# Second attention layer of a graph network: scores turned first, border rows stored by SyncE, queries spread as two float32r parts

## The reference, cut to what matters

```python
xn = _layernorm(x, ln1_g, ln1_b)
q = (xn @ Wq + bq).reshape(n, H, DH)
k = (xn @ Wk + bk).reshape(n, H, DH)
v = (xn @ Wv + bv).reshape(n, H, DH)
ep = ef @ We + be
scores = jnp.einsum('ehd,ehd->eh', q[dst], k[src] + ep[:, None, :]) * scale
scores = scores * ew[:, None]
m = jax.ops.segment_max(scores, dst, num_segments=n)
ex = jnp.exp(scores - m[dst])
s = jax.ops.segment_sum(ex, dst, num_segments=n)
attn = ex / s[dst]
out = jax.ops.segment_sum(attn[:, :, None] * v[src], dst, num_segments=n)
```

## Time and profile before

| what | value |
|---|---|
| time, median of 3 (lowest, highest) | 7788.41 us (7787.7, 7788.8) |
| profiled execution, span from first to last instruction | 7783.9 us |
| busy in the span: PE, DVE, ACT, POOL | 73%, 61%, 47%, 67% |
| granted TensorE clock, mean of the span | 0.852 |

### The profile page before, as it was taken

The page is one execution under the profiler, slowest core; times in us unless marked ns, Lnnn a source line. Parts: engine busy times, 40 slices in busy tenths (PEclk is TensorE's granted clock), DMA queues, the critical chain, the costliest instruction groups (busy, mean ns, idle before and its releaser), DMA issues. The chain is left out here.

```text
span 7783.9 us, 119247 instructions
## 1 busy us (share of the span) xinstructions
PE 5677.2 (73%) x30906; PEld 4272.7 (55%) x30906; DVE 4785.2 (61%) x14720; ACT 3689.1 (47%) x11072; POOL 5222.5 (67%) x5181
## 2 busy tenths in 40 slices
PE   6777765555568989968999999798555555667764
PEld 5666665555545666645666666565433434545543
DVE  8666666666657888867889898411222223555555
ACT  1333332222257777745777787342000002777774
POOL 4777777777777777734777777211777773777773
PEclk9777787777789999988999999898777777888787
DMA  4333241111156665546666666322444443444444
GB/s 148 79 76 81 77 107 36 37 36 33 36 125 154 159 159 154 156 114 167 190 187 188 186 190 177 111 66 78 109 109 108 109 108 72 110 110 110 109 109 89
DMA packets 1041439, 886.68 MB, mean 114 GB/s; under 512 B 748889, under 2 KB 857457, under 8 KB 1040663
## 3 DMA queue, kind: packets, MB, share of 16 engines
q0 software_dynamic: 259600, 658.46, 30.8%
q1 hardware_dynamic: 725907, 162.47, 10.7%
q10 hardware_dynamic: 55284, 58.13, 2.2%
HBM read 737.69 MB, written 140.99 MB: 113 GB/s over the span
## 5 line engine op out<-in xcount | busy, mean ns | idle before, releaser
L1282 POOL DMA_INDIRECT edges_kv<-kv,edges_rec x1712 | 1882.4, 1100 | 639.2 <-issue 525.9
L1428 PE MATMUL banks<-edges_kv,edges_hot 128*128 128x288 f32 (+2 forms) x5136 | 1484.8, 438 | 322.7 <-DVE edges_kv L1752 234.1
L1428 PEld LDWEIGHTS banks<-edges_kv,edges_hot 128*128 128x128 f32 x5136 | 1030.9, 209 | 605.8 <-issue 336.2
L1943 POOL DMA_INDIRECT edges_rows<-rel,edges_rec x856 | 809.5, 946 | 382.2 <-issue 255.6
L572 POOL DMA_INDIRECT by_src_records<-sort_by_src_rec,sort_by_src_pos_i x808 | 795.5, 985 | 325.6 <-issue 226.5
L1282 POOL DMA_INDIRECT edges_kv<-feat,edges_rec x856 | 828.9, 968 | 268.5 <-issue 245.2
L1959 PE MATMUL banks<-edges_rows,edges_hot 128*128 128x256 f32 x1712 | 625.0, 529 | 467.7 <-DMA edges_rows<-rel,edges_rec 431.3
L572 POOL DMA_INDIRECT by_dst_records<-sort_by_dst_rec,sort_by_dst_pos_i x808 | 787.6, 975 | 246.4 <-issue 243.6
L659 DVE SCALAR_TENSOR_TENSOR sort_junk<-banks,sort_hot_lo 128x128 bf16<-128x128 f32 x1616 | 437.9, 287 | 654.5 <-PE banks L721 638.6
L1959 PEld LDWEIGHTS banks<-edges_rows,edges_hot 128*128 128x128 f32 x1712 | 429.6, 263 | 663.5 <-DMA edges_rows<-rel,edges_rec 269.3
L1582 ACT ACTIVATE edges_off<-columns,edges_column 128x128 bf16<-128x128 f32 x2568 | 785.6, 393 | 0.0
(11 more groups left out here) (433 smaller groups left out, 11669.2 us busy)
## 6 DMA issues: line engine op xcount, KB each, us to landing
edges_kv<-kv,edges_rec POOLq DMA_INDIRECT x1712
sort_feat<-in_edge_attr_dram SPq DMA_DIRECT2D x100, 256.0 KB, 4.0
rel<-tables_stage SPq DMA_DIRECT2D x100, 252.0 KB
by_dst_records<-by_dst_blank ACTq DMA_DIRECT2D x21, 800.0 KB
edges_rec<-by_dst_records SPq DMA_DIRECT2D x26, 640.0 KB, 7.0
by_src_records<-by_src_blank ACTq DMA_DIRECT2D x1, 13696.0 KB, 52.6
edges_rows<-rel,edges_rec POOLq DMA_INDIRECT x856, 2.7
edges_kv<-feat,edges_rec POOLq DMA_INDIRECT x856
```

Of the source, the lines that this page charges most:

```text
L1282: pool.indirect_dma_start(kv[:, r, c, 0:koff + DIM], None, tab, bass.IndirectOffsetOnAxis(ap=reci[:, b, c, idx:idx + 1], axis=0)).then_inc ...
L1428: last = pe.matmul(ps[:, 6 + m % 2, 0:OW], hot[:, b % 2, c, :], kv[:, b % BUFS, c, koff:koff + OW], start=(c % 2 == 0), stop=(kind != 1 an ...
L1943: pool.indirect_dma_start(rows[:, r, c, :], None, tab, bass.IndirectOffsetOnAxis(ap=reci[:, b, c, idx:idx + 1], axis=0)).then_inc(gathered ...
```

## The change

Three things change in the second layer, and some tiles share memory to make place for them.

1. TensorE's `body` turns the scores of the step before first, then does `with_past` of pair 3 (of three steps before; it was the last thing of the body of the step ahead), and then `expand` of pair 2.
2. Border rows are stored in every step by SyncE (`store_ends`), `STORE_LAG` = 9 steps behind the step for which it loads; `HELD` is 2 for this layer. ScalarE waits, ahead of a step's first pair, for the store of two steps earlier.
3. Queries come in two parts: `q_high`, with the low 12 bits of each word cleared, and the rest in `x`. `hot_t` is float32r, and `expand` makes two float32r products per tile, one with each part, into the same PSUM columns. `join_and_project` makes the parts, two VectorE instructions more per block.

Beside that, records are loaded with 37 words in place of 40, five small tiles of the layer lie in `by_src.cont_all`, tiles of the joining part lie in `h` and `hn`, and `acc1` lies in the memory of `acc0`.

```diff
+F32R = mybir.dt.float32r
+HIGH_BITS = -(1 << 12)
...
-    RW = O.width - word0
+    RW = (O.words["weight"] + 1 if kind == 1 else O.width) - word0
...
-    HOT = F32 if kind < 3 else BF16
+    HOT = (F32, F32R, None, BF16)[kind]
...
-    HELD = 4
+    HELD = 2 if kind == 1 else 4
+    STORE_LAG = 9
...
+                ends_rows = C.ends[0:T, 0:OW].rearrange("(i q) w -> q i w", q=2)
+
+                def store_ends(j, b):
+
+                    sp.wait_ge(sums_copied, at(j, b)(PAIRS, PAIRS))
+                    sp.dma_start(ends_rows[:, bass.ds(at(j, b)(PAIRS, 0), PAIRS), :],
+                                 pair_sums[BN:P, b % HELD]).then_inc(ends_kept[b % HELD], 16)
 
                 def body(j, b):
+                    load(j, b)
+                    stored = before(j, b, STORE_LAG)
+                    if kind == 1 and stored:
+                        store_ends(*stored)
+
+                def load(j, b):
...
-                        rows = q[:, bass.ds(blocks[m], 1), :].rearrange("p o w -> p (o w)")
+                        rows = [part[:].bitcast(F32R)[:, bass.ds(blocks[m], 1), :].rearrange("p o w -> p (o w)") for part in q]
...
                         for c in range(2):
-                            last = pe.matmul(out[:, c, :], hot_t[:, b % 2, 2 * m + c, :], rows, start=True, stop=True,
-                                             skip_group_check=True)
+                            for part in range(2):
+                                last = pe.matmul(out[:, c, :], hot_t[:, b % 2, 2 * m + c, :], rows[part], start=(part == 0), stop=(part == 1),
+                                                 skip_group_check=True)
...
+                    gone = lagging(j, b, 3)
+                    if older:
+                        turn_scores(*older)
+                    if gone:
+                        with_past(*gone, 3)
                     if inside:
                         expand(j, b, (2,))
-                    if older:
-                        turn_scores(*older)
...
-                    if oldest and kind == 1:
-                        with_past(*oldest, 3)
...
-                    if 0 in pairs and b % HELD == 0:
+                    if kind == 1 and 0 in pairs and not first_steps(j, b, HELD):
+                        act.wait_ge(ends_kept[b % HELD], (j * (UNROLL // HELD) + b // HELD) * 16)
+                    if kind != 1 and 0 in pairs and b % HELD == 0:
                         act.wait_ge(ends_out, j * (UNROLL // HELD * 16) + b // HELD * 16)
...
-                    if PAIRS - 1 in pairs and (b % HELD == HELD - 1 or b == size(j) - 1):
+                    if kind != 1 and PAIRS - 1 in pairs and (b % HELD == HELD - 1 or b == size(j) - 1):
...
                     dve.tensor_tensor(x[:, b, :], ps[:, Q_BANK[b % 2], 0:DIM], bias[:, KV:KV + DIM], ALU.add).then_inc(q_kept, 1)
+                    dve.wait_ge(q_kept, b + 1)
+                    dve.tensor_scalar(q_high[:, b, :].bitcast(I32), x[:, b, :].bitcast(I32), HIGH_BITS, None, ALU.bitwise_and).then_inc(q_cut, 1)
+                    dve.wait_ge(q_cut, 2 * b + 1)
+                    dve.tensor_tensor(x[:, b, :], x[:, b, :], q_high[:, b, :], ALU.subtract).then_inc(q_cut, 1)
```

More of the change, by code:

```diff
@@ L1100, in blocks_of, with edge_layer @@
     return [((word >> (5 * m)) & 31).with_bounds(min_val=0, max_val=NB - 1) for m in range(PAIRS)]
-def edge_layer(nc, C, L, label, tab, q, acc, w_attr=None, beside=None):
+def edge_layer(nc, C, L, label, tab, q, acc, w_attr=None, beside=None, spare=None):
     kind, H, O, koff = L.kind, L.heads, L.order, L.koff
@@ L1188, in edge_layer @@
         pen = ph.sbuf("pen", [HG, 3, P + 1])
[L1189 to L1193, removed]
+        names = ("run_max", "seg_max", "last_max", "below", "expo")
+        run_max, seg_max, last_max, below, expo = (spare[0:HG, P * i:P * i + P] if spare else ph.sbuf(name, [HG, P])
+                                                   for i, name in enumerate(names))
         score = ph.sbuf("score", [P, G, H])
@@ L1236, in edge_layer @@
         ends_out = ph.sem("ends_out")
+        ends_kept = [ph.sem(f"ends_kept{i}") for i in range(HELD)] if kind == 1 else None
         added = ph.sem("added")
@@ L1256, in body @@
                     sp.dma_start(rec[:, b:b + some].rearrange("p s c w -> p (s c) w"),
-                                 records[:, bass.ds(j * (UNROLL * G) + b * G, some * G), word0:O.width]).then_inc(rec_in[b // LOAD], 16)
+                                 records[:, bass.ds(j * (UNROLL * G) + b * G, some * G), word0:word0 + RW]).then_inc(rec_in[b // LOAD], 16)
                     if beside and (j, b) == (1, 0):
@@ L1268, in _ @@
                 steps(sp, body)
+                if kind == 1:
+                    for n in range(STEPS - STORE_LAG, STEPS):
+                        store_ends(n // UNROLL, n % UNROLL)
+                    for i in range(HELD):
+                        sp.wait_ge(ends_kept[i], 16 * len(range(i, STEPS, HELD)))
                 if beside:
@@ L2062, in split_tiles, with split_views @@
         self.node_row = sbuf("node_row", [P, TB * P])
+    def split_views(self, L, first, second, sbuf):
+        H, n = L.heads, TB * P
+        self.cont_pen, self.max_row = first[0:H, 0:n + 1], first[0:H, n + 1:2 * n + 1]
+        self.run_max, self.node_row = second[0:H, 0:n], second[:, n:2 * n]
+        self.factor = sbuf("factor", [P, TB, H])
+        self.below = sbuf("below", [P, TB, H])
 FAR_BANKS = (3, 6, 7)
@@ L3278, in build @@
         far0, far1, far3 = (far for _, far in C.far_tables)
-        H0 = 16
-        kv0 = table("kv0", NR, P + DIM)
-        L = Layer(0, H0, by_src, P, P)
-        with nc.sbuf_tensor("acc0", [P, NB, L.out_width], F32) as acc:
+        H0, H1 = 16, 8
+        kv0, kv1 = table("kv0", NR, P + DIM), table("kv1", NR, 2 * DIM)
+        x_kept, h_kept = (nc.dram_tensor(name, (P, NB, DIM), F32, kind="Internal").ap() for name in ("x1_kept", "h1_kept"))
+        L0, L1 = Layer(0, H0, by_src, P, P), Layer(1, H1, by_dst, DIM, DIM)
@@ L3285, in build @@
+        with nc.sbuf_tensor("acc0", [P, NB, L0.out_width], F32) as acc0:
+            acc1 = acc0[:].rearrange("p b w -> p (b w)")[:, 0:NB * L1.out_width].rearrange("p (b w) -> p b w", b=NB)
             with nc.sbuf_tensor("q0", [P, NB, P], F32) as q, nc.sbuf_tensor("w_attr", [P, 2, 2 * P], F32) as w_attr:
[L3286 removed]
+                sort_all(nc, C, A, x, by_src, by_dst, table("edge_projected", E, 32), kv0, q, acc0, w_attr,
@@ L3296, in build @@
-        L = Layer(1, H1, by_dst, DIM, DIM)
-        with nc.sbuf_tensor("acc1", [P, NB, L.out_width], F32) as acc:
-            edge_layer(nc, C, L, "edges1", kv1, x, acc)
+                edge_layer(nc, C, L0, "edges0", kv0, q, acc0, w_attr, by_dst)
+            with nc.sbuf_tensor("q1_high", [P, NB, DIM], F32) as q_high:
+                join_and_project(nc, C, L0, "tables1", far0, acc0, x, q_high, kv1, x_kept, h_kept, (A["L1_gnn_ln1_g"], A["L1_gnn_ln1_b"]),
+                                 [(A[f"L1_gnn_W{c}"], A[f"L1_gnn_b{c}"]) for c in "qkv"], A["L1_gnn_be"], (DIM // H1) ** -0.5, H1)
+                edge_layer(nc, C, L1, "edges1", kv1, (q_high, x), acc1, spare=by_src.cont_all)
```

17 lines of the change are left out of this document (6 added, 11 removed).

## The result

The changed kernel takes **7707.24 us** (median; 7701.76 to 7714.56 in 4 runs) beside 7788.6 us for the kernel before: ratio 0.9895, interval 0.9883 to 0.9907, 81 us less. The profiled execution has a span of 7712.8 us, 71.1 less than that of before; forecast were 7715 us and a span of 7710.9.

The account below looks back on a forecast made before the run. The prediction took TensorE and ScalarE handing each other work as the bound: 106 x (12.17 - 11.40) = 82 us less, 9 more for splitting, hence 7715 us, likeliest case 7699 to 7733, with cases from 7676 to 7760 taken in.

Parts of the forecast that it names:

- The ring of TensorE and ScalarE: Second layer: the two engines hand each other work, bounding an undisturbed step at 11.78 us; the mean is 12.17.
- Store, 0.39 per step: Border rows stored by SyncE end ScalarE's wait for the store: 0.39 us per step gained, between 0 and 0.45.
- The lead of the record loads: SyncE's record loads go out about one step later, but eight steps ahead of use, so their readers should not feel it.
- Turn, 0.11 and not 75 us: Turning scores first takes a 0.11 us slot off the TensorE-ScalarE path; VectorE's 75.0 us of waits are not counted.
- Float32r at the cheap end: Query spreading: float32r streams like bfloat16, 0.114 us per 256 columns, 0.46 per pair, so 0.40 less for pair 2.
- The hot matrix limits: Products cannot start until 0.34 us after ScalarE's hot matrix, done at 4221.10, so the step closes at 11.40 us.
- The other three pairs are worth nothing: Spreading for pairs 0, 1 and 3 lies beside ScalarE's chain, so making it cheaper gains nothing.
- Splitting, 9 us: Stage before the layer: two more VectorE instructions per block, about 0.8 us, unhidden in 11 of 25 blocks: 9 us.
- holding is elastic: GpSimd's gathers wait out a key addition, others fall between: 10.0 us of work fits an 11.40 step, 1.4 may be lost.
- The 12.4 us: GpSimd's step if four VectorE instructions with two SBUF inputs each hold gathers by half; then no gain in the layer.
- the rival that leant on "HAM oscillation": TensorE busy only 84%, its clock falls to 0.81, the step grows to 12.27 us, 7808 us in all; chance 0.06.
- Sum: 106 steps, each from 12.17 to 11.40 us, give 82 us less; splitting adds 9: 73 less, span 7710.9, median 7715.

Follow-up runs that it names:

- turn late: Changed kernel with the turn of the scores back behind the spreading of pair 2: 11.48 us per step, ratio 0.9902.
- pair 2: Changed kernel with one float32 product per tile, in place of two float32r, for the third of four spread pairs only: 11.75 us per step, ratio 0.9944.
- spreading first: Changed kernel with the query spreading of pair 2 ahead of the past of pair 3: 11.30 us per step, ratio 0.9890; again 11.29, 0.9881.
- short key additions: Changed kernel with VectorE's two key additions per step replaced by adding a constant, without the second SBUF input: 11.40 us per step, ratio 0.9892.
- pairs 0, 1 and 3 in float32: Changed kernel with one float32 product per tile for these three spread pairs, the remaining pair in float32r: 11.52 us per step, ratio 0.9921.
- turn alone: Kernel before with only TensorE's new order, scores turned ahead of pair 3's past and pair 2's spreading: 12.15 us per step, ratio 0.9978.
- both: Changed kernel with pair 2's spreading ahead of pair 3's past and key additions replaced by adding a constant: 11.29 us per step, ratio 0.9877.

## Why the prediction was right, and where not

- *The ring of TensorE and ScalarE is the bound; 106 times 12.17 is the number to beat.* Shown: edits on the ring (turn late, pair 2, spreading first) change the step by their own length or by what the hot matrix leaves of it, and an edit off it (short key additions) by nothing; the one off it that counted (pairs 0, 1 and 3 in float32) closed another way around.
- *Store, 0.39 per step.* Measured 0.36; the stall is gone, and SyncE's wait behind it costs nothing. The lead of the record loads is not the eight steps of the prediction: a load goes out some 63 us, 5.5 steps, ahead of the first gather of its steps (7.2 steps in the kernel before); it lands in 7.6 us, and nobody waits for it.
- *Turn, 0.11 and not 75 us.* Measured 0.10 (the step with the store, without and with the turn) and 0.11 (turn late). With the turn alone the wait moved to the spread queries, as said.
- *Float32r at the cheap end.* Right: 0.117 us apart where 0.114 was taken, and 0.57 for pair 2 where 0.56 was. A float32 product took 0.43 by the prediction's reading (0.96 for a pair, less 0.1 of filling), 3.7 times as long; that agrees with the Trainium skill, "FP8 and Floating Point Precision", section "TensorE Precision Notes", by which true float32 makes four passes.
- *The hot matrix limits: the products not before 0.34 us after its end, ring 11.40.* This step failed in size. The 0.34 came from the past of pair 3, which follows ScalarE's copy by that; the products follow the hot matrix by 0.05 when nothing else holds them (spreading first). So in the changed kernel the hot matrix does not limit; copy, past, spreading and products in a row do. By that row alone the prediction's own terms give 4221.31 - 4210.04 = 11.27, and the median distance of two score reductions is 11.30 us. (Nor does the sum lose a tenth of the float32r gain to the hot matrix, as it says, but 0.13 of 0.40, a third.) Longer ones, most of all at the layer's two ends (12.72, 13.16 and 13.01), bring the mean to 11.375. That this lies near 11.40 is luck, two errors against each other: the ring closes 0.1 earlier, and the length of a plain step was put where the sum needs a mean.
- *The other three pairs are worth nothing.* Wrong by 0.15 us per step, 16 us. In float32 they would have kept the products waiting for VectorE's weighing, a way around the step that the prediction did not follow. The sum came out all the same, as in the changed kernel no pair was left in float32.
- *Splitting, 9 us.* Measured 5.8: 17 us of instructions, not 20, with 11.2 hidden.
- *The gathers: holding is elastic.* Right, and the gathers fill the step whatever its length: 8 x (859.4 + 236.4)/776 = 11.30 us in the changed kernel, 8 x (861.5 + 240.5)/776 = 11.36 with short key additions, 11.22 with both, with almost no wait for buffers. The trace shows the holding itself (rows in the last section): a long gather starts beside a key addition or a weighing and ends 0.8 us after it, as the prediction read from one row. Its reading that a weighing holds for only 0.57 - 0.30 us fell, for a gather inside a weighing ends 0.8 us after it too. That agrees with the Trainium skill, "SBUF — State Buffer", section "SBUF: two separate sides", by which the one that comes second is blocked until the other's whole instruction is over. The 12.4 us that the prediction worked out from it did not come: the gathers meet four such instructions per step, but only about two of eight are held, 1.3 us in all. When the key additions became short, other gathers were held, some of them by the short additions with their one SBUF input, and so the mean stayed.
- *The clock.* It rose to 1.00 (the 2.4 GHz level) with TensorE busy for 86% of the stretch, and did not fall; the rival that leant on "HAM oscillation" in "TensorE: Matmul & The Clock Gate" of the Trainium skill did not come about. TensorE's longest wait for ScalarE in the stretch (L1460) was 1.6 us.
- *Sum.* Forecast -82 in the layer and +9 ahead of it; measured -84.5 and +4.5 in the traces. The median stands 81 us below that of before. That the span came within 2 us (7712.8 for 7710.9) is in part luck: layer and splitting gave 7 us more than forecast, and the stages that the change does not touch took 8.9. The forecast kept the median 4.5 us above the span; it lies 5.6 below, as the profiled execution (7714.56 us) was the slowest of the four.

## What to carry to other kernels

Look for the ring: two engines that each wait for the other, step after step, set the time here even beside a third that is busy for 97%. A wait of an engine outside that ring, however long in the list of waits, is worth only what its removal shortens in the ring: 75 us of waiting were worth 11 here. When a part is called free, follow every input of the next work in the ring, and ask which comes last once the first is earlier; and price how one engine follows another from the same pair of instructions.

## What was not expected

Three of the four spread pairs, off the ring in every row of the kernel before, cost 0.15 us per step in float32, through VectorE's weighing. And the gathers: with a VectorE instruction that reads one SBUF operand, the mean gather did not become shorter (1110 ns for 1107), and it kept GpSimd as full as before:

```profile
4215.46 1.50 POOL L1302 DMA_INDIRECT edges_kv<-kv,edges_rec  x1 [0.30 <-issue]
4217.27 1.59 POOL L1302 DMA_INDIRECT edges_kv<-kv,edges_rec  x1 [0.30 <-issue]
4219.16 0.95 POOL L1302 DMA_INDIRECT edges_kv<-kv,edges_rec  x1 [0.30 <-issue]
```

This is GpSimd with short key additions: two gathers of each eight take 1.5 to 1.6 us, where the changed kernel has one of 2.01 and one of 1.1 to 1.3. VectorE beside the first two, a weighing and a short key addition:

```profile
4214.93 1.22 DVE L1777 TENSOR_TENSOR edges_kv<-edges_kv 128x1024 f32<-128x1024 f32 x1
...
4217.36 0.68 DVE L1804 TENSOR_SCALAR edges_kv<-edges_kv 128x1024 f32<-128x1024 f32 x1
```

The gathers end at 4216.96 and 4218.86, 0.81 and 0.82 us after these two. In the changed kernel, GpSimd and then VectorE's key addition and weighing:

```profile
4213.48 2.01 POOL L1302 DMA_INDIRECT edges_kv<-kv,edges_rec  x1 [0.30 <-issue]
4215.79 0.94 POOL L1302 DMA_INDIRECT edges_kv<-kv,edges_rec  x1 [0.31 <-issue]
4217.04 1.14 POOL L1302 DMA_INDIRECT edges_kv<-kv,edges_rec  x1 [0.30 <-issue]
```

```profile
4213.45 1.21 DVE L1804 TENSOR_TENSOR edges_kv<-edges_kv,edges_rec 128x1024 f32<-128x1024 f32 x1
...
4216.15 1.21 DVE L1777 TENSOR_TENSOR edges_kv<-edges_kv 128x1024 f32<-128x1024 f32 x1
```

The first and the third gather end 0.83 and 0.82 us after them. All 191 gathers of the stretch that take more than 1.05 us stand beside a key addition or a weighing and end 0.81 to 0.83 us after it; with short key additions 234 of 240 stand so. A gather that starts in the midst of a weighing is held in 94 of 97 cases of the changed kernel. Of those that start ahead of such an instruction, or within 0.05 us of its beginning, some are held and most take 0.95; what decides that, no run shows.

The lost time of eight gathers, 8 x 1.11 - 8 x 0.95 = 1.3 us per step, is the same in both kernels.
